# Reordering the weight preparation around the first chain of powers, and moving Wo's low half

## The chip, the cores and the metric

One core of a Trainium2 chip runs the whole kernel. The metric is the device time of one execution, in microseconds. The profiled execution, from which all rows come, is one more execution of the same kernel.

## What is computed

The input x is 4 batches of 512 tokens by 512 numbers, the context 4 by 512 by 256. In short:

```python
q = ln(heads(layernorm(x) @ Wq + bq))            # 16 heads of 32
k, v = heads(y_main @ Wk + bk), heads(y_main @ Wv + bv)      # 496 context tokens
kd, vd = heads(y_dca @ Wkv_dca + bkv_dca)                    # the last 16 tokens
x = x + (attn(q, ln(k), v) + attn(q, ln(kd), vd)) @ Wo + bo
h = silu(layernorm(x) @ lut[gate_idx].T) * (layernorm(x) @ lut[up_idx].T)
x = x + h @ lut[down_idx].T                       # inner width 1376, lut of 16 numbers
```

Every head of q and k is normalised over its 32 numbers, so there are sixteen inverse roots for each token.

## The kernel before

**Precision.** Each matrix product runs in two halves: an operand is a float16 high part plus a float16 low part, and three products (high by high, high by low, low by high) are summed. So every weight is first centred where a head norm follows (Wq, Wk and the key half of Wkv_dca: VectorE sums the heads and subtracts the mean), then converted to the high half by ScalarE, then its low half is made by a subtraction on VectorE (`low`) or, for Wv, on POOL (`values_low`, lines 495 to 498).

**The engines** run one program each, written out in order. Semaphores connect them, and whatever stands behind a waiting instruction on its engine waits too. `core` (each engine has one) is a batch's attention in numbered slots, and `between(slot)` or `prepare(slot)` hangs other work into the slots:

- Slots 0 to 8 are the projections. Eight units u (four query tiles, then the key tiles 1, 2, 3, 0) each go: TensorE `project(u)`; ScalarE `square`; VectorE `variance` (a sum for each head, L861); POOL `rstd(u)` (the power -1/2, L524); VectorE `normalise` (L867); TensorE `turn_heads` (four transposes, L1231); ScalarE `rescale` (L634, L636); VectorE `low_half` (L876). In slot u TensorE issues project(u+1), then turn_heads(u-1). VectorE issues variance(u+1), normalise(u), low_half(u-1), then the slot's extra. POOL issues rstd(u+1) and then its extra. Unit 7 is key tile 0: its 16 first tokens are the separate ones, so it takes 14 key matmuls and 12 value matmuls, a copy of the context split in two (POOL's `split_context`, whose ready signal is c0_set), and both halves of Wkv_dca (L1207, wait for wd_lo).
- Slots 9 to 40 (S_ONE on) are the first score stage: 32 pairs of heads, for the row maxima (VectorE L918, L919) and the sums of exponentials (ScalarE L664).
- Slots 41, 42 make the shifts, and slots 43 to 58 (S_TWO on) are the second score stage, 16 of them: transposed scores, exponentials (ScalarE L690), products with the values (TensorE L1305), and the norm and turn of the next batch's x.

**The lookups.** During batch 0 the FFN's weights are built from the indices, in 33 chunks. The indices come as int32 into four staging buffers (SP: `load_idx`), POOL casts a block of three chunks to float16 (`convert`, L464), SP stores it in HBM (`store_idx`) and, once a buffer is free, loads the index block four further on, then reads each chunk back in the shape needed (`load_rep`). VectorE makes four one-hot arrays of a chunk (L780), TensorE multiplies by the table (`look_up`, L1154), ScalarE evacuates (L591, L592). One chunk goes with every second slot of the first score stage, then one with each slot of the second. `load_rep(c)` waits until the one-hot set of chunk c-2 is made. EARLY says how many blocks are cast and stored before the first copies are read: POOL's `prepare` (L555) casts blocks 0 and 1 in slots 4 and 5 and the rest from S_ONE on, one for each slot.

SP's queue after its first loads (lines 346 to 364) is:

```python
for it in range(STAGES): load_idx(it)
for it in range(EARLY):  store_idx(it)
load_rep(0); load_rep(1)
sp.wait_ge(s["wd_lo"], 1)
sp.dma_start(st_o.rearrange("p (k n) -> p k n", k=G), by_chunk("Wo")).then_inc(s["wo_in"], 16)
for c in range(2, NCH):
    if EARLY + c - 2 < IT: store_idx(EARLY + c - 2)
    ...
    load_rep(c)
```

POOL begins with four requests for the lookup table (L430), then constants (lines 431 to 448), the roots for the first x tiles, the selectors, the table's constants, Wv's low half, the root for x tile 2, and then its core. In POOL's core, `split_context` stands in slot 2 behind rstd(3), and `shift_patterns` (three casts, L477 to L479) at S_ONE + 2.

Batches 1 and 2 run in a loop with the FFN of the batch before hung into the slots. Batch 3 and its FFN follow it.

## Time and profile before

| | us |
|---|---|
| median of 3 runs | 907.59 |
| lowest and highest | 905.56, 909.68 |
| the profiled execution's own time | 908.92 |
| span of the profiled execution | 907.1 |
| mean granted TensorE clock in it | 0.964 |
| TensorE matmuls busy | 799.5 (88%) |
| VectorE busy | 522.1 (58%) |
| ScalarE busy | 487.4 (54%) |
| POOL busy | 240.8 (27%) |

The own time is what the device counts for the execution, the span what the profiler's records cover. Shares of busy time are means over stages with different limits. The granted clock is TensorE's, in parts of 2.4 GHz. In the rows, PE is TensorE, DVE VectorE, ACT ScalarE, and an arrow in square brackets names what ended the idle time that stands before it. In tile names, `arena` is a large buffer that is cut into many tiles, `ps` is PSUM.

### The profile page before, as it was taken

Reading aid. Unit: us, or ns where it says so; the run is one execution under the profiler, and the core shown is the slowest. Engines: PE = TensorE matmul, PEld = TensorE weight load, DVE = VectorE, ACT = ScalarE, POOL = GpSimd, SP = SyncE. Lnnn points to the kernel's source line nnn. Section 1 sums busy time; section 2 is a strip of 40 time slices with the busy share of each in tenths; the row PEclk is TensorE's granted clock in tenths of the full one; section 3 lists DMA queues with packets and bytes.
Section 4 is the critical chain, followed back from the end, with each engine's and each line's share of the span. In section 5 each row is a group of like instructions: output and inputs, shape, how many; then the busy total and the mean of one; then the engine's idle time right before and its main releaser. Section 6 shows DMA issues by size and latency. Waiting matters only on the chain.

```text
span 907.1 us, 15618 instructions
## 1 busy us (share of the span) xinstructions
PE 799.5 (88%) x5892; PEld 319.0 (35%) x5892; DVE 522.1 (58%) x934; ACT 487.4 (54%) x964; POOL 240.8 (27%) x284
## 2 busy tenths in 40 slices
PE   3756666699889999999899999999999999979998
PEld 1321122233345333332444333334443332234443
DVE  7759999687564888221646984216458940052220
ACT  3456567677335788554246886652558865511100
POOL 7693100000156222100472222003732210002320
PEclk9986688899999999999999999999999999999999
DMA  8349844354400000112000000101000000000001
GB/s 266 98 135 293 222 131 111 90 143 117 134 1 0 2 1 1 36 47 59 26 1 1 1 1 24 48 24 47 1 1 1 1 24 25 24 24 1 1 7 40
DMA packets 45098, 50.08 MB, mean 55 GB/s; under 512 B 5984, under 2 KB 33120, under 8 KB 45024
## 3 DMA queue, kind: packets, MB, share of 16 engines
q1 hardware_dynamic: 44688, 48.81, 18.5%
q8 instruction: 49, 0.80, 0.4%
q10 hardware_dynamic: 208, 0.26, 0.1%
q14 instruction: 25, 0.20, 0.1%
q0 software_dynamic: 128, 0.00, 0.0%
HBM read 40.61 MB, written 8.45 MB: 54 GB/s over the span
## 4 chain that ended last, share of the span: by engine, by line
PE 41%; issue 26%; DVE 17%; POOL 7%; ACT 7%; DMA 1%; DVEq 0%; POOLq 0%; SPq 0%; ACTq 0%
PE ps L1108 29%; DVE arena L780 5%; DVE nmax L918 4%; PE ps L1305 3%; PE ps L1288 3%; PE ps L1261 3%; ACT ps L664 3%; POOL hrstd L524 2%; ACT arena L690 2%; POOL xrstd L492 1%; POOL arena L487 1%; PE ps L1154 1%; DVE arena L919 1%; DMA arena<-in_x 1%; DVE stat L811 1%
## 5 line engine op out<-in xcount | busy, mean ns | idle before, releaser
L1108 PE MATMUL ps<-arena,wf_hi 128*128 128x512 f16 (+1 forms) x704 | 211.9, 383 | 4.3 <-DVE arena L787 1.6
L664 ACT ACTIVATE ps<-ps,nmax 128x496 f32<-128x496 f32 x256 | 165.0, 645 | 67.1 <-DVE arena L919 66.0
L690 ACT ACTIVATE arena<-ps 128x1024 f32<-128x1024 f32 x128 | 125.4, 1023 | 78.9 <-PE ps L1294 78.8
L918 DVE TENSOR_REDUCE nmax<-ps 128x2 f32<-128x992 f32 x128 | 151.9, 1187 | 22.7 <-PE ps L1261 22.7
L1108 PE MATMUL ps<-arena,wf_lo 128*128 128x512 f16 (+1 forms) x352 | 134.2, 381 | 0.0
L524 POOL TENSOR_TENSOR hrstd<-hvar,mhalf 128x16 f32<-128x16 f32 x32 | 93.8, 2932 | 134.1 <-DVE hvar L861 134.0
L1108 PE MATMUL ps<-wf_hi,arena 128*128 128x512 f16 (+1 forms) x352 | 114.1, 380 | 0.1
L1108 PEld LDWEIGHTS ps<-arena,wf_hi 128*128 128x128 f16 (+1 forms) x704 | 66.5, 100 | 93.0 <-DVE arena L787 11.1
L780 DVE TENSOR_SCALAR arena<-arena,wf_lo 128x2048 f16<-128x2048 f16 (+1 forms) x132 | 94.1, 779 | 6.3 <-DMA arena<-idx 3.7
L1154 PE MATMUL ps<-arena,wf_lo 128*32 128x512 f16 (+1 forms) x1056 | 76.5, 432 | 22.8 <-ACT wf_lo L592 21.2
L492 POOL TENSOR_TENSOR xrstd<-xvar,mhalf 128x1 f32<-128x1 f32 x32 | 18.0, 564 | 267.4 <-DVE xvar L816 267.2
L1261 PE MATMUL ps<-arena 32*128 32x512 f16 x768 | 56.9, 401 | 22.5 <-ACT ps L664 11.5
L618 ACT ACTIVATE arena<-ps 128x512 f32<-128x512 f32 x32 | 19.2, 599 | 96.3 <-PE ps L1108 95.2
L1305 PE MATMUL ps<-arena 128*32 128x512 f32 x512 | 68.2, 604 | 0.0
L1108 PE MATMUL ps<-wf_lo,arena 128*128 128x512 f16 (+1 forms) x176 | 66.7, 379 | 0.0
L422 POOL TENSOR_TENSOR idle<-mhalf 128x1 f32<-128x1 f32 x52 | 10.0, 193 | 204.9 <-DVE arena L795 204.4
L800 DVE SCALAR_TENSOR_TENSOR arena<-ps,arena 128x512 f32<-128x512 f32 x16 | 11.1, 692 | 87.3 <-PE ps L1108 87.3
L1108 PE MATMUL ps<-wq,arena 128*128 128x512 f16 x192 | 47.4, 397 | 14.5 <-DVE arena L867 6.5
L1108 PEld LDWEIGHTS ps<-wf_hi,arena 128*128 128x128 f16 (+1 forms) x352 | 34.3, 97 | 69.0 <-issue 31.6
L599 ACT ACTIVATE arena<-ps 128x512 f32<-128x512 f32 (+1 forms) x44 | 26.4, 601 | 56.9 <-PE ps L1108 56.9
L1288 PE MATMUL ps<-arena 32*128 32x512 f16 x768 | 52.9, 378 | 3.6 <-ACT arena L690 3.6
L1154 PEld LDWEIGHTS ps<-arena,wf_lo 128*32 128x32 f16 x1056 | 27.8, 106 | 72.5 <-ACT wf_lo L592 35.0
(135 smaller groups left out, 1027.4 us busy)
## 6 DMA issues: line engine op xcount, KB each, us to landing
arena<-idx SPq DMA_DIRECT2D x124, 128.0 KB, 2.8
arena<-in_x SPq DMA_DIRECT2D x32, 256.0 KB, 2.9
wf_lo<-in_idx SPq DMA_DIRECT2D x10, 512.0 KB, 5.6
out<-arena SPq DMA_DIRECT2D x16, 256.0 KB, 2.0
idx<-wf_hi SPq DMA_DIRECT2D x10, 384.0 KB, 3.2
wf_lo<-in_idx SPq DMA_DIRECT2D x11, 256.0 KB, 6.3
arena<-in_ctxT SPq DMA_DIRECT2D x4, 512.0 KB, 5.0
arena<-in_Wq SPq DMA_DIRECT2D x4, 256.0 KB, 6.7
```

The costliest lines, as they stand in the source:

```text
L492: pool.tensor_tensor(xrstd[:, kind - 1, i:i + 1], xvar[:, kind - 1, i:i + 1], mhalf[:, 0:1], ALU.pow).then_inc(s[f"rstd{kind}"], 1)
L524: pool.tensor_tensor(hrstd[:, u % 2, :], hvar[:, u % 2, :], mhalf[:, :], ALU.pow).then_inc(s["hrstd_set"], 1)
L599: act.activation(sg[it % 2][0:m, :], ps[0:m, FB, :], ACT.Tanh, scale=0.5 / WS).then_inc(s["tanh_set"], 1)
L664: last = act.activation(sc, sc, ACT.Exp, bias=nmax[:, 0, t, h:h + 1], accum_out=den[:, 0, t, h:h + 1])
L690: act.activation(probs[n_ % 2][:, 2 * p:2 * p + 2, :], ps[:, bank:bank + 2, :], ACT.Exp).then_inc(s["probs_set"], 1)
L780: dve.tensor_scalar(l_oh[q][:, 0:n_], l_rep[c % 2][:, 0:n_], l_j[:, q:q + 1], None, ALU.is_equal)\
L918: dve.tensor_reduce(nmax[:, 0, t, 2 * p:2 * p + 2], sc[:, :, DCA:S], AX_X, ALU.max, negate=True)
L1108: last = pe.matmul(dst, l, r, start=(first and i == 0), stop=(stop and i == len(todo) - 1))
L1154: last = pe.matmul(ps[g * 32:(g + 1) * 32, FB + a_, 0:w], l_c[a_][:, q, :], l_oh[q][:, g * w:(g + 1) * w], start=(q == 0), stop=(q == NJ - ...
L1261: last = pe.matmul(ps[:, pair_bank(m + j // 2) + j % 2, :], qT[x_][of_head(j), g, cols], kT[y_][of_head(j), g, :], start=(k == 0), stop=(k ...
L1288: pe.matmul(ps[:, SC + j, :], kT[x_][of_head(j), g, cols], qT[y_][of_head(j), g, :], start=(k == 0), stop=False)
L1305: last = pe.matmul(ps[j * HD:(j + 1) * HD, AB, :], v_sb[:, kt, h * HD:(h + 1) * HD], probs[n_ % 2][:, j, :], start=(kt == 0), stop=(kt == ...
```

## The change

Each engine's list is reordered. No arithmetic is added or removed.

- SP: Wq's third block is loaded ahead of x tile 1. One block instead of two is stored ahead of the first copies. Wo's load waits for two signals of wd_lo (Wkv_dca's low half is now in two parts).
- POOL: the requests for the table stand behind the constants. Wv's low half moves behind rstd(1), the split of the context behind rstd(4). Block 0 is cast in slot 1, block 1 in slot 8, blocks 2 to 10 from slot 9 on, and the shift patterns in slot S_ONE + 12.
- ScalarE: Wv's high half moves behind b's. The turn of x tile 3 stands ahead of Wk's high half. Wkv_dca's conversion is in slot 3 instead of 2. The wait for the value bias moves to Wo's conversion.
- VectorE: the low half of x tile 0 stands earlier. The sums and centring of Wk stand later, with the low half of x tile 3 between. Wk's low half is in slot 0. Wkv_dca's low half is made in two parts in slots 4 and 5 instead of whole in slot 3. Wo's low half is in slot S_TWO + 2 instead of S_ONE + 8.
- TensorE: unit 7 waits for both parts of Wkv_dca's low half.

```diff
-STAGES, EARLY = 4, 2
+STAGES, EARLY = 4, 1
@@ SP
-                if k == 1:
+                if k == 2:
                     load_x(1, tile_of(flat, xaddr(0, 0, 1)), x_first[1])
...
-            sp.wait_ge(s["wd_lo"], 1)
+            sp.wait_ge(s["wd_lo"], KC)
@@ POOL
-            for r in range(NR4):
-                pool.dma_start(lut_w[r * 32:(r + 1) * 32, :], row("lut", r * NJ, (r + 1) * NJ).to_broadcast([32, NJ])).then_inc(s["lut_in"], 16)
             pool.memset(mhalf[:, :], -0.5).then_inc(s["ident_set"], 1)
...
             pool.memset(caug[:, :, :, :, :, :].rearrange("p t j e w c -> p (t j e w c)"), 0.0).then_inc(s["caug_zero"], 1)
+            for r in range(NR4):
+                pool.dma_start(lut_w[r * 32:(r + 1) * 32, :], row("lut", r * NJ, (r + 1) * NJ).to_broadcast([32, NJ])).then_inc(s["lut_in"], 16)
...
-                    if u == 2:
+                    if u == 3:
                         split_context(a)
...
             lookup_constants()
-            values_low()
             norm(1, 2, (0, 0))
             def prepare(slot):
-                if 4 <= slot < 4 + EARLY:
-                    convert(slot - 4)
-                if slot == S_ONE + 2:
+                if slot == 0:
+                    values_low()
+                if slot == 1:
+                    convert(0)
+                if NU <= slot < NU + IT - EARLY:
+                    convert(EARLY + slot - NU)
+                if slot == S_ONE + 12:
                     shift_patterns()
-                if S_ONE <= slot < S_ONE + IT - EARLY:
-                    convert(EARLY + slot - S_ONE)
@@ ScalarE
                 if prev is None:
                     act.wait_ge(s["par_set"], 1)
-                    act.wait_ge(s["bvs_set"], 1)
...
             query_hi(1)
+            query_hi(2)
             turn(1, 1, (0, 0), LB0[1])
-            act.wait_ge(s["wv_in"], 16)
-            act.activation(fl(wv[0]), st_kv[1], ACT.Copy, scale=WS).then_inc(s["wv_hi"], 1)
-            query_hi(2)
             query_hi(3)
             act.activation(b16[:, :], st_b, ACT.Copy, scale=WS).then_inc(s["b_hi"], 1)
+            act.wait_ge(s["wv_in"], 16)
+            act.activation(fl(wv[0]), st_kv[1], ACT.Copy, scale=WS).then_inc(s["wv_hi"], 1)
...
             turn(1, 2, (0, 0), LB0[2])
+            turn(1, 3, (0, 0), LB0[3])
             act.wait_ge(s["wk_cent"], 1)
             act.activation(fl(wk[0]), st_kv[0], ACT.Copy, scale=WS).then_inc(s["wk_hi"], 1)
-            turn(1, 3, (0, 0), LB0[3])
             def prepare(slot):
-                if slot == 2:
+                if slot == 3:
                     act.wait_ge(s["wd_cent"], 1)
...
                 if slot == S_ONE + 3:
+                    act.wait_ge(s["bvs_set"], 1)
                     act.wait_ge(s["wo_in"], 16)
@@ VectorE
-            moments(1, 1, first, x_first[1])
             query_centre(1)
             query_low(0)
+            moments(1, 1, first, x_first[1])
+            turn(1, 0, first, LB0[0])
             query_sums(2)
             standardise(1, 1, first, x_first[1], x_first[1])
             query_centre(2)
             query_low(1)
-            turn(1, 0, first, LB0[0])
...
             standardise(1, 2, first, x_first[2], x_first[2])
-            dve.wait_ge(s["wk_in"], 16)
-            dve.tensor_reduce(sum_k, key, A-_-, ALU.add).then_inc(s["wk_sum"], 1)
             moments(1, 3, first, x_first[3])
             variance(first, 1)
             turn(1, 2, first, LB0[2])
+            standardise(1, 3, first, x_first[3], x_first[3])
+            normalise(first, 0, True)
+            dve.wait_ge(s["wk_in"], 16)
+            dve.tensor_reduce(sum_k, key, A+_+, ALU.add).then_inc(s["wk_sum"], 1)
+            turn(1, 3, first, LB0[3])
             dve.wait_ge(s["wk_sum"], 1)
             dve.scalar_tensor_tensor(out=key, in0=spread(sum_k), scalar=-1.0 / HD, in1=key, op0=ALU.mult, op1=ALU.add).then_inc(s["wk_cent"], 1)
-            standardise(1, 3, first, x_first[3], x_first[3])
-            normalise(first, 0, True)
...
-            turn(1, 3, first, LB0[3])
-            dve.wait_ge(s["wk_hi"], 1)
-            low(fl(wk[1]), st_kv[0], fl(wk[0])).then_inc(s["wk_lo"], 1)
...
                 if slot == 0:
                     dve.tensor_tensor(bvs[:, :], bvm, bvd, ALU.add).then_inc(s["bvs_set"], 1)
+                    dve.wait_ge(s["wk_hi"], 1)
+                    low(fl(wk[1]), st_kv[0], fl(wk[0])).then_inc(s["wk_lo"], 1)
...
-                if slot == 3:
+                if slot in (4, 5):
                     dve.wait_ge(s["wd_hi"], 1)
-                    low(wd[1][:, :, :], st_d, wd[0][:, :, :]).then_inc(s["wd_lo"], 1)
-                if slot == S_ONE + 8:
+                    k = slot - 4
+                    low(wd[1][:, k, :], st_d[:, k, :], wd[0][:, k, :]).then_inc(s["wd_lo"], 1)
+                if slot == S_TWO + 2:
                     dve.wait_ge(s["wo_hi"], 1)
                     low(fl(wo[1]), st_o, fl(wo[0])).then_inc(s["wo_lo"], 1)
@@ TensorE, unit 7
-                            pe.wait_ge(s["wd_lo"], 1)
+                            pe.wait_ge(s["wd_lo"], KC)
```

## Rows read from the trace of the kernel before

**Rows 1.** Stages: us; busy of PE, PEld, DVE, ACT, POOL; clock, DMA, GB/s.

```profile
68.50:161.00 92.50, 56.21 (x672) 17.51 (x672) 90.99 (x139) 61.51 (x162) 11.30 (x8) 0.77 0.66 185
...
170.00:238.90 68.90, 64.46 (x928) 22.36 (x928) 53.14 (x92) 53.69 (x76) 2.21 (x4) 1.00 0.45 121
...
238.90:907.10 668.20, 636.51 (x4075) 259.73 (x4075) 326.67 (x597) 339.38 (x677) 174.66 (x210) 0.99 0.06 19
```

**Rows 2.** Timeline of POOL, front: start us, us, line, operation.

```profile
1.26 2.21 POOL L430 DMA_DIRECT2D wf_lo<-in_lut  x4 [0.82 <-POOLq L1355]
...
20.64 1.49 POOL L497 TENSOR_SCALAR arena<-arena 128x1024 f32<-128x1024 f32 x1
...
22.21 2.12 POOL L498 TENSOR_TENSOR wv<-arena,wv 128x1024 f16<-128x1024 f32 x1
...
28.26 2.91 POOL L524 TENSOR_TENSOR hrstd<-hvar,mhalf 128x16 f32<-128x16 f32 x1
...
38.22 5.83 POOL L524 TENSOR_TENSOR hrstd<-hvar,mhalf 128x16 f32<-128x16 f32 x2 [7.05 <-DVE hvar L861]
...
46.90 2.91 POOL L524 TENSOR_TENSOR hrstd<-hvar,mhalf 128x16 f32<-128x16 f32 x1 [0.36 <-DVE hvar L861]
...
54.38 1.46 POOL L464 CAST wf_hi<-wf_lo 128x1536 f16<-128x1536 int32 x1
...
60.52 3.34 POOL L524 TENSOR_TENSOR hrstd<-hvar,mhalf 128x16 f32<-128x16 f32 x1
```

**Rows 3.** Timeline of VectorE, front.

```profile
24.89 0.55 DVE L821 TENSOR_SCALAR arena<-arena,mv,xrstd 128x512 f32<-128x512 f32 x1 [1.79 <-POOL xrstd L492]
...
34.50 0.69 DVE L833 TENSOR_TENSOR arena<-ps,arena 128x512 f16<-128x512 f32 x1 [2.67 <-ACT arena L603]
...
37.44 0.70 DVE L861 TENSOR_REDUCE hvar<-arena 128x16 f32<-128x528 f32 x1
...
48.55 2.29 DVE L967 SCALAR_TENSOR_TENSOR wd<-arena,wd 128x2048 f16<-128x2048 f32 x1
...
55.07 1.32 DVE L876 TENSOR_TENSOR arena<-arena 128x512 f16<-128x512 f32 x1
```

**Rows 4.** Timeline of TensorE, front.

```profile
28.84 4.34 PE L1108 MATMUL ps<-wq,arena 128*128 128x512 f16 x12 [2.69 <-DVE arena L833]
...
35.25 2.76 PE L1108 MATMUL ps<-wq,arena 128*128 128x512 f16 x12 [0.98 <-DVE arena L833]
...
47.47 0.66 PE L1231 MATMUL ps<-ident,arena 128*128 128x128 f32 x4 [1.97 <-DVE arena L867]
...
64.64 1.12 PE L1231 MATMUL ps<-ident,arena 128*128 128x128 f32 x4 [4.06 <-DVE arena L867]
```

**Rows 5.** Two windows of one us: columns as in rows 1.

```profile
30.00:31.00 1.00, 1.00 (x4) 0.36 (x3) 1.00 (x3) 1.00 (x1) 1.00 (x1) 0.50 0.04 10
...
32.00:33.00 1.00, 1.00 (x6) 0.39 (x4) 0.00 (x0) 0.00 (x0) 0.00 (x0) 0.97 0.00 0
```

**Rows 6.** Timelines of VectorE and POOL, first score stage.

```profile
72.41 2.73 DVE L780 TENSOR_SCALAR arena<-arena,wf_lo 128x2048 f16<-128x2048 f16 x4
...
77.44 3.90 DVE L780 TENSOR_SCALAR arena<-arena,wf_lo 128x2048 f16<-128x2048 f16 x4
...
77.35 1.47 POOL L464 CAST wf_hi<-wf_lo 128x1536 f16<-128x1536 int32 x1 [5.66 <-DMA wf_lo<-in_idx]
...
95.29 2.28 DVE L967 SCALAR_TENSOR_TENSOR wo<-arena,wo 128x2048 f16<-128x2048 f32 x1
...
97.49 1.18 DVE L918 TENSOR_REDUCE nmax<-ps 128x2 f32<-128x992 f32 x1
```

**Rows 7.** Line 780, 77.4 to 81.2: ns least, median, most.

```profile
L780 DVE TENSOR_SCALAR arena<-arena,wf_lo x4: 737/742/1919, 77.4 to 80.6; 128x2048 f16<-128x2048 f16 x4
```

**Rows 8.** Timelines of VectorE and TensorE, second score stage.

```profile
181.28 2.73 DVE L780 TENSOR_SCALAR arena<-arena,wf_lo 128x2048 f16<-128x2048 f16 x4
...
187.07 2.49 PE L1154 MATMUL ps<-arena,wf_lo 128*32 128x512 f16 x32
```

More of the change, by code:

```diff
@@ L1025, in _ @@
             standardise(1, 2, first, x_first[2], x_first[2])
-            dve.wait_ge(s["wk_in"], 16)
-            dve.tensor_reduce(sum_k, key, AX_X, ALU.add).then_inc(s["wk_sum"], 1)
             moments(1, 3, first, x_first[3])
@@ L1030, in _ @@
             turn(1, 2, first, LB0[2])
+            standardise(1, 3, first, x_first[3], x_first[3])
+            normalise(first, 0, True)
+            dve.wait_ge(s["wk_in"], 16)
+            dve.tensor_reduce(sum_k, key, AX_X, ALU.add).then_inc(s["wk_sum"], 1)
+            turn(1, 3, first, LB0[3])
             dve.wait_ge(s["wk_sum"], 1)
             dve.scalar_tensor_tensor(out=key, in0=spread(sum_k), scalar=-1.0 / HD, in1=key, op0=ALU.mult, op1=ALU.add).then_inc(s["wk_cent"], 1)
-            standardise(1, 3, first, x_first[3], x_first[3])
-            normalise(first, 0, True)
             dve.wait_ge(s["ln_in"], 16 * len(PARAMS))
```

## The prediction

> **What bounds the kernel now.** I read the stages first, then each engine's timeline in the stretches that the change touches. The stages [rows 1] show that the edited program (batch 0 and the lookups) is 238.9 us of 907.1, and that TensorE is 64.46 of 68.9 us busy in the second score stage and 636.51 of 668.2 us behind it. That last stretch is untouched. In the first score stage (68.5 to 161) VectorE is busy 90.99 of 92.5 us, and it is the bound. In front of it runs the chain of powers on POOL. From rstd(2) on, each of the two engines waits for the other by turns.
>
> The powers take 2.9 us each [rows 2]. The third starts only at 38.22, after a wait of 7.05 for VectorE's sum, itself at 37.44 [rows 3]. The sixth ends at 54.38, where the first index cast starts. The eighth starts at 60.52 and ends at 63.86, and the first scores follow at 68.5 [rows 1].
>
> **The sum, part 1: the front.** The lut requests (2.21 us on POOL [rows 2]) leave the head, but x0's root must still pass them: I take 0, at most 2.2 gained. The reordered Wq2/x1 loads and the earlier x turn shift VectorE by under 1 us. The real gain is Wv's low half (1.49 + 2.12 us [rows 2]) leaving the path of rstd of x2: the step behind that root waited 1.79 us for it, until 24.89 [rows 3], and can now run near 22.4. Following VectorE's new order with unchanged durations, projection 2 can start at about 25.95 rather than 28.84, and x3's low half at about 30.2 rather than 34.50 [rows 3].
>
> Between that low half and the sum for rstd(2) there were 2.94 us of VectorE work (34.50 to 37.44). Now Wk's centring (1.13) and the parameters (0.9) come on top, with about 1 us of waiting for ScalarE's conversion of Wk. The sum's end would be at 36.1, 2.0 earlier than 38.14. But Wv's low half now starts on POOL when rstd(1) ends, about 28.8, and its two-input step runs from 30.4 to 32.5, just when the centring of Wk wants to start. In the row at 55.07 a VectorE step with two SBUF inputs took 1.32 instead of 0.68 us, until the cast of 54.38 (1.46) had ended [rows 2, 3]. By that the centring waits until 32.5 and the sum ends at 37.8. If projection 2 finds the low clock (12 matmuls in 4.34 rather than 2.76 us [rows 4], 0.50 granted, which is 1.2 GHz [rows 5]) it also ends at about 37.7. I take 37.8; bounds 36.1 and 38.2.
>
> From there POOL has rstd(2), the conversion of block 0 (1.46), rstd(3), rstd(4), the split of the context, rstd(5). The split took 2.5 us, from 44.05 (the two powers from 38.22) to 46.54, which is 46.90 less its wait of 0.36. With hand-offs that is 4 x 2.9 + 1.46 + 2.6 = 15.7, so rstd(5) ends at 53.5 (bounds 51.8 and 53.9), against 54.38. All their inputs come earlier: the costliest is ScalarE's Wkv_dca conversion, now a slot later, and I find the fifth sum ready near 47.4 while POOL is free near 50.7.
>
> Now the new wait. Projection 7 (the mixed tile) waits for both parts of Wkv_dca's low half, and the second stands in slot 5, behind normalise(5), which waits for rstd(5). The whole low half was 2.29 us and ended at 50.84, ahead of need [rows 3]. Now: 0.05 + 0.6 (normalise) + 0.6 (low half 4) + 1.15 = 2.4 us after rstd(5), about 55.9, TensorE may start. It will have been idle for over 6 us. After 4.06 idle four transposes took 1.12 us, after 1.97 idle 0.66 [rows 4]. The projection's 14 key matmuls cost 3.2 us at the rate of the row at 35.25 (2.76 for 12) and about 4.8 us if the first 3.2 us are at half rate, as in the row at 28.84, where 0.50 was granted until about 32 [rows 4, 5]. I take 4.9 with hand-off: they end at 60.8. ScalarE's square 0.65, VectorE's sum 0.75, and rstd(7) starts at 62.3: later than 60.52, though its two casts are gone from between. The values' 12 matmuls (2.6), transposes, ScalarE's rescales of units 5, 6 (1.35 each) and 7 (1.9) and VectorE's low halves between them put the scores 9.3 us after the keys' end: 70.1. Casts of blocks 1 to 4 run on POOL right then and may hold a low half back by 0.6 (it did at 55.07). **Front: +1.7** (scores at 70.2); the ends are 66.8 (-1.7: 51.8 and the high clock) and 71.4 (+2.9: every low half held).
>
> **Part 2: first score stage.** VectorE loses Wo's low half: 97.49 - 95.29 = -2.2 us, all of it on the bound [rows 6]. Its cover is full: no idle is shown from 72.4 to 161. What comes on: a one-hot set of four takes 2.73 us alone and 3.90 when an index cast runs beside it (77.35 against 77.44) [rows 6]. A single instruction of it then takes 1.92 instead of 0.74 [rows 7]. Four of the five casts after 72.41 collided (sets of 77.44, 83.66, 89.91, 99.02); the fifth, at 103.85, ended before 105.27. So 4 x 1.2 = 4.8 us lie in this stage today. With EARLY at 1, load 5 is issued one chunk later and so are those behind it. The casts in this stage become 5 to 10, six, and the three casts of the shift patterns (0.6, 0.2 and 1.0 us, in front of the stage till now) come behind the tenth. A load is issued when a set has ended, and its cast starts 9 to 10 us after that end; a cycle is 2.4 + 2.65 to 3.9, so two cycles later the next set is under way: the phase makes collisions the rule. I take 0.6 for the first, 5 x 1.2 for the rest and 0.5 of the patterns: 7.1 against 4.8, **+2.3**, bounds -4.8 (none) and +3.9 (8.7 in all). SP's other moves (Wo behind the second part of Wd's low half, one store fewer ahead of the first copies) leave the first copies earlier, at about 44, and nothing waits for them: a set could not start before its slot.
>
> **Part 3: second score stage.** The 2.2 us of Wo's low half now stand ahead of the set that ran 181.28 to 184.01 [rows 8]. TensorE's lookup of 187.07 took 2.49 rather than 1.91 us: it is already at VectorE's heels, and otherwise dense [rows 1, 8]. With the set 2.2 later the lookup in front of it ends about 1.4 late, the set of 186.16 and its lookup 2.0 late. TensorE has no gap behind to win it back, and transfers start from the sets, so they shift too. **+2.0**; bounds 0 and 2.2. The 79 per cent busy VectorE speaks for 0; where it is idle it waits for TensorE, so I stay near 2.
>
> ScalarE's wait for bvs moves to a slot where it is long met: 0. Sum: +1.7 - 2.2 + 2.3 + 2.0 = **+3.8 us**. On the profiled execution's 908.9 that is 912.7; on the median of the three runs, 907.6 (the profiled one is 1.3 above it), 911.4. I forecast 911.4. A measurement tells about 0.5 per cent, 4.5 us.
>
> **A page on it.** The Trainium skill, "SBUF — State Buffer", section "Who interferes with whom", says that VectorE and GpSimd share one port pair as an exclusive lock: fast-mode and two-input VectorE work and GpSimd's reads shut each other out for whole instructions. By that rule whatever of the moved casts meets such work costs its full length, the patterns' casts and the low halves of the tail too, and the sum would be that of the first rival, 914.2; the rows at 55.07 and 77.44 agree with it for the casts that they show [rows 3, 6].
>
> **The rivals.** *Lock everywhere (slower)*: place, the casts. If loads land so that every cast and pattern meets a set, and the tail's low halves too, front +2.9 and stage one +3.9 - 2.2, stage two +2.0: +6.6, 914.2, over the bound. For it: four collisions of five today. Against: the fifth missed. It decides from about five collisions plus the patterns on.
> *The chain leads (no change)*: Wk's centring starts before POOL's step (it misses by 0.4 us), and TensorE's clock stays high: front -1.7, else as forecast: +0.4, 908.0. Against: six idle microseconds before projection 7.
> *Casts miss (faster)*: no cast meets a set: 4.8 saved, -2.2, +2.0, +1.7 = -3.3, 904.3; with the chain leading as well 900.9, past the bound on the other side. For it: the phase depends on when the loads land, and the cast of 103.85 missed. Against: 4 of 5.
> *Wo hidden*: the second stage absorbs it: 909.4.
> The change can hardly fail to do what it says: each line moves work in a fixed order.
>
> **How the numbers follow.** Forecast 0.45; lock everywhere 0.25; chain leads 0.12; casts miss 0.10 (half of that past the bound); Wo hidden 0.08. The range for eight in ten runs from the chain-leads case less the runs' own scatter of 2 us, 905.5, to the lock case and as much, 916. Slower by over 0.5 per cent: the lock case nearly whole and a quarter of the forecast's, 0.34. Faster: 0.08. Same: 0.58.
>
> **What would show it.** Right: rstd(2) near 37.8; TensorE idle over 5 us before the 14 matmuls of projection 7, at a granted clock of 0.50, with Wkv_dca's second low half just before; rstd(7) after 62; first scores at 70; six 1.9-us one-hot instructions in stage one; a lookup 2 us late from 187 on. Wrong: scores before 68, fewer than four long one-hots, or the stage from 170 no longer than 68.9 us.

## The result, and the profile after

| | before | changed |
|---|---|---|
| median of the runs | 907.18 (14 runs) | 914.54 (14 runs) |
| lowest to highest | 902.45 to 909.68 | 910.18 to 917.63 |
| span of the first trace | 907.1 | 910.1 |
| span of a second trace | 904.1 | 916.0 |

The ratio is 1.0079 with a 95% interval of 1.0061 to 1.0096: slower by 7.3 us, 0.8 per cent. The slowest run of the kernel before (909.68) still lies below the fastest of the changed one (910.18). The forecast was 911.4 in a range of 905.5 to 916.

Three places on TensorE cut the run into stages: the first scores, the four transposes of the shifts (at the end of the first score stage), and the first projection of the second batch. TensorE's timeline of the changed kernel, with the key matmuls of unit 7 ahead of them:

```profile
55.12 2.72 PE L1110 MATMUL ps<-wk,arena 128*128 128x512 f16 x6 [5.30 <-DVE wd L968]
...
57.63 2.27 PE L1110 MATMUL ps<-wd,arena 128*128 128x512 f16 x6
...
71.84 1.47 PE L1263 MATMUL ps<-arena 32*128 32x512 f16 x12 [3.44 <-DVE arena L877]
...
166.51 0.58 PE L1278 MATMUL ps<-ident_h,caug 128*128 128x128 f16 x4 [7.88 <-DVE caug L942]
...
241.48 2.76 PE L1110 MATMUL ps<-wq,arena 128*128 128x512 f16 x12 [1.37 <-ACT wf_lo L593]
```

The same places in the kernel before:

```profile
52.59 1.46 PE L1108 MATMUL ps<-wk,arena 128*128 128x512 f16 x6
...
68.51 1.47 PE L1261 MATMUL ps<-arena 32*128 32x512 f16 x12 [2.75 <-DVE arena L876]
...
165.09 0.58 PE L1276 MATMUL ps<-ident_h,caug 128*128 128x128 f16 x4 [7.88 <-DVE caug L941]
...
238.96 2.76 PE L1108 MATMUL ps<-wq,arena 128*128 128x512 f16 x12 [1.37 <-ACT wf_lo L592]
```

With the second traces of both (runs `after_again` and `before_again` below), the stages last, in us:

| | front | first score stage | second score stage | rest |
|---|---|---|---|---|
| before | 68.5, 66.2 | 96.6, 94.9 | 73.9, 73.8 | 668.1, 669.2 |
| changed | 71.8, 73.6 | 94.7, 97.5 | 75.0, 75.8 | 668.6, 669.1 |
| difference of the means | +5.4 | +0.3 | +1.6 | +0.2 |

The sum, +7.5, is what the medians show. One pair of traces alone would have misled: the first pair gives +3.0. Two other runs that share the changed kernel's whole front, `wo_back` and `sp_early2`, have it at 73.4 and 73.3.

**The front.** VectorE's timeline of the changed kernel: the centring of Wk, the second part of Wkv_dca's low half, and the last three low halves of the projections:

```profile
29.18 2.87 DVE L1036 SCALAR_TENSOR_TENSOR arena<-arena 128x1024 f32<-128x1024 f32 x1
...
53.75 1.22 DVE L968 SCALAR_TENSOR_TENSOR wd<-arena,wd 128x1024 f16<-128x1024 f32 x1
...
64.92 1.71 DVE L877 TENSOR_TENSOR arena<-arena 128x512 f16<-128x512 f32 x1 [2.63 <-ACT arena L637]
...
67.16 1.34 DVE L877 TENSOR_TENSOR arena<-arena 128x512 f16<-128x512 f32 x1
...
70.41 1.38 DVE L877 TENSOR_TENSOR arena<-arena 128x512 f16<-128x512 f32 x1 [1.91 <-ACT arena L637]
```

And POOL's: Wv's low half (second step), the third power, the eighth, the casts behind it:

```profile
28.84 2.13 POOL L498 TENSOR_TENSOR wv<-arena,wv 128x1024 f16<-128x1024 f32 x1
...
36.23 2.90 POOL L524 TENSOR_TENSOR hrstd<-hvar,mhalf 128x16 f32<-128x16 f32 x1 [5.25 <-DVE hvar L862]
...
61.77 2.90 POOL L524 TENSOR_TENSOR hrstd<-hvar,mhalf 128x16 f32<-128x16 f32 x1 [6.39 <-DVE hvar L862]
...
64.62 6.62 POOL L464 CAST wf_hi<-wf_lo 128x1536 f16<-128x1536 int32 x4
```

The third power starts at 36.23, 2.0 earlier than the 38.22 of [rows 2], although the centring was held up: 2.87 us at 29.18, until the step of 28.84 (2.13) had ended. Against the second trace of the kernel before, where this power starts at 35.95, it is no lead at all. Whatever lead there is, it is lost. The second part of Wkv_dca's low half ends at 54.97, and only then do unit 7's key matmuls start, at 55.12. They take 2.72 and 2.27 us for six each where they took 1.46 before. TensorE had stood idle for 5.30 us, and the clock granted to it is 0.50, which is 1.2 GHz. Its windows say so (columns as in rows 1, the clock is the third from the end):

```profile
55.00:57.00 2.00, 1.89 (x5) 0.74 (x6) 0.00 (x0) 0.00 (x0) 0.38 (x1) 0.50 0.41 49
57.00:59.00 2.00, 2.00 (x6) 0.70 (x5) 0.00 (x0) 0.00 (x0) 0.00 (x0) 0.50 0.93 345
```

The eighth power waits until 61.77. Behind it four casts run from 64.62, and the three low halves beside them take 1.71, 1.34 and 1.38 us instead of 0.7.

**The first score stage.** VectorE's timeline of the changed kernel, three sets of one-hot arrays:

```profile
80.79 2.73 DVE L781 TENSOR_SCALAR arena<-arena,wf_lo 128x2048 f16<-128x2048 f16 x4
...
99.50 2.74 DVE L781 TENSOR_SCALAR arena<-arena,wf_lo 128x2048 f16<-128x2048 f16 x4 [2.22 <-DMA arena<-idx]
...
105.66 2.74 DVE L781 TENSOR_SCALAR arena<-arena,wf_lo 128x2048 f16<-128x2048 f16 x4 [1.03 <-DMA arena<-idx]
```

The long sets of [rows 6] are gone: all but one (3.10 at 116.72) take the plain 2.73 us in the first trace, where 4.8 us of blocking had been (two sets, of 3.24 and 3.04 us, are longer in the second trace). Instead three sets wait for their copies, 3.7 us in all (2.22, 1.03, 0.43), and in the second trace four sets, 5.4. SP's queue shows why, load 5's second part and then the next requests:

```profile
66.97 0.70 SPq L312 DMA_DIRECT2D wf_lo<-in_idx  x1
...
78.50 2.86 SPq L330 DMA_DIRECT2D arena<-idx  x4
...
92.26 3.03 SPq L312 DMA_DIRECT2D wf_lo<-in_idx  x1
```

SP issued nothing from 67.7 to 78.50. The store of block 2 and load 6 stood behind the copies of chunk 2, which wait for the first set. The windows show the transfers (columns as in rows 1; the last two are the DMA share and GB/s):

```profile
71.80:78.40 6.60, 3.72 (x36) 0.91 (x40) 5.06 (x9) 2.73 (x8) 1.47 (x1) 0.50 0.00 0
78.40:105.00 26.60, 16.13 (x208) 5.35 (x204) 23.56 (x39) 18.16 (x46) 4.08 (x3) 0.85 0.98 259
```

Nothing moves for 6.6 us, and then the DMA engines are full for 26 (a share of 0.98). The issue of one kind of request (line 312) grows as well, from 0.70 us at 66.97 to 3.03 at 92.26.

**The second score stage.** VectorE's timeline, Wo's low half and the set behind it, and TensorE's, the two lookups that use this set and the next:

```profile
182.92 2.28 DVE L968 SCALAR_TENSOR_TENSOR wo<-arena,wo 128x2048 f16<-128x2048 f32 x1
...
185.12 2.73 DVE L781 TENSOR_SCALAR arena<-arena,wf_lo 128x2048 f16<-128x2048 f16 x4
...
186.02 2.51 PE L1156 MATMUL ps<-arena,wf_lo 128*32 128x512 f16 x32 [0.81 <-DVE arena L781]
...
190.90 2.51 PE L1156 MATMUL ps<-arena,wf_lo 128*32 128x512 f16 x32 [0.40 <-DVE arena L781]
```

Both lookups waited for VectorE. In the kernel before only the second of the two was held ([rows 8]), and by half a microsecond.

### The profile page after: what moved, and what is told of

Its sections match the earlier page's. It is cut to its first block, busy times and chain, and to the rows that moved or that the text cites. A ratio compares the mean times of both kernels' runs of the same rounds, so it can differ in the third digit from the quotient of the medians.

```text
span 910.1 us, 15619 instructions
## 1 busy us (share of the span) xinstructions
PE 802.8 (88%) x5892; PEld 320.6 (35%) x5892; DVE 522.2 (57%) x935; ACT 487.1 (54%) x964; POOL 238.5 (26%) x284
## 4 chain that ended last, share of the span: by engine, by line
PE 42%; issue 26%; DVE 14%; ACT 8%; POOL 6%; DMA 2%; SPq 1%; DVEq 0%; POOLq 0%; ACTq 0%
PE ps L1110 30%; ACT ps L664 4%; PE ps L1307 3%; PE ps L1290 3%; PE ps L1263 3%; DVE arena L781 3%; DVE nmax L919 2%; POOL hrstd L524 2%; PE ps L1156 2%; ACT arena L690 2%; POOL xrstd L492 1%; DMA wf_lo<-in_idx 1%; POOL arena L487 1%; PE ps L1233 1%; DVE stat L812 1%
## 5 line engine op out<-in xcount | busy, mean ns | idle before, releaser
L664 ACT ACTIVATE ps<-ps,nmax 128x496 f32<-128x496 f32 x256 | 165.2, 646 | 66.2 <-DVE arena L920 65.0
L1110 PEld LDWEIGHTS ps<-arena,wf_hi 128*128 128x128 f16 (+1 forms) x704 | 66.6, 101 | 93.3 <-DVE arena L788 11.0
L781 DVE TENSOR_SCALAR arena<-arena,wf_lo 128x2048 f16<-128x2048 f16 (+1 forms) x132 | 89.6, 740 | 9.3 <-DMA arena<-idx 6.9
L1263 PE MATMUL ps<-arena 32*128 32x512 f16 x768 | 55.6, 393 | 23.4 <-ACT ps L664 11.7
L1307 PE MATMUL ps<-arena 128*32 128x512 f32 x512 | 68.2, 604 | 0.0
L422 POOL TENSOR_TENSOR idle<-mhalf 128x1 f32<-128x1 f32 x52 | 10.1, 194 | 205.1 <-DVE arena L796 204.6
L1290 PE MATMUL ps<-arena 32*128 32x512 f16 x768 | 53.5, 381 | 3.3 <-ACT arena L690 3.3
L1156 PEld LDWEIGHTS ps<-arena,wf_lo 128*32 128x32 f16 x1056 | 28.0, 106 | 71.8 <-ACT wf_lo L593 31.2
```

Of the source, the lines that this page charges most:

```text
L664: last = act.activation(sc, sc, ACT.Exp, bias=nmax[:, 0, t, h:h + 1], accum_out=den[:, 0, t, h:h + 1])
L781: dve.tensor_scalar(l_oh[q][:, 0:n_], l_rep[c % 2][:, 0:n_], l_j[:, q:q + 1], None, ALU.is_equal)\
L1110: last = pe.matmul(dst, l, r, start=(first and i == 0), stop=(stop and i == len(todo) - 1))
L1156: last = pe.matmul(ps[g * 32:(g + 1) * 32, FB + a_, 0:w], l_c[a_][:, q, :], l_oh[q][:, g * w:(g + 1) * w], start=(q == 0), stop=(q == NJ - ...
L1263: last = pe.matmul(ps[:, pair_bank(m + j // 2) + j % 2, :], qT[x_][of_head(j), g, cols], kT[y_][of_head(j), g, :], start=(k == 0), stop=(k ...
L1290: pe.matmul(ps[:, SC + j, :], kT[x_][of_head(j), g, cols], qT[y_][of_head(j), g, :], start=(k == 0), stop=False)
```

## The experiments

All times are medians; the ratio is to the kernel before, run on the same chip, with its 95% interval.

**`after_again`, `before_again`: no edit.** For the changed kernel:

> The changed kernel once more, for a second trace and a joint comparison. The median of its runs was 7.3 us over the kernel before (914.5 against 907.2), while its trace shows only 3.0 us (span 910.1 against 907.1): front +3.3, first score stage -1.9, second +1.1, rest +0.5. Theory A (the trace shown is a lucky execution: the first stage's collisions and copy waits differ from one execution to the next): this trace shows a front within 0.5 us of the last and a first stage several us longer. Theory B (the difference lies elsewhere, in the loop and the last batch): the first stage again lasts 94.7 us, and the rest behind the second stage differs. Time: about 914.

Measured: 915.4 (1.0080, 1.0057 to 1.0104), span 916.0. Stage one lasts 97.5 instead of 94.7, as theory A has it. But the front is not the same within 0.5 us: it is 1.8 longer. TensorE's timeline of this trace:

```profile
56.03 2.72 PE L1110 MATMUL ps<-wk,arena 128*128 128x512 f16 x6 [6.58 <-DVE wd L968]
...
58.54 2.77 PE L1110 MATMUL ps<-wd,arena 128*128 128x512 f16 x6
...
73.64 1.47 PE L1263 MATMUL ps<-arena 32*128 32x512 f16 x12 [3.43 <-DVE arena L877]
```

The second part of Wkv_dca came 0.9 us later, and twelve matmuls rather than some ten ran at the low clock (2.72 and 2.77). The 0.9 us arose on POOL: beside VectorE's two-input steps at 48.64 and 49.44, the last step of the split took 0.65 us instead of 0.22, and rstd(5) 3.87 instead of 3.34. For the kernel before:

> The kernel before once more, for a second trace of it. Its one trace (span 907.1) lies 1.7 us above what its median of 907.2 stands for (the own time is 1.8 above the span), and the changed kernel's two traces (910.1 and 916.0) lie 2.6 below and 3.2 above the median's 912.8. Theory, the casts' phase varies from execution to execution: this trace has the same front (first scores within 0.5 us of 68.5), but fewer than four long one-hot sets or a first stage other than 96.6 us by over 1. Rival, the kernel before is regular and the kernels differ elsewhere: again four long sets, first stage 96.6, and the whole within 1 us of 907.1.

Measured: 906.45 (1.0006, 0.9988 to 1.0024), span 904.1. One long set instead of four, a wait of 1.4 for a copy, and stage one 94.9: the phase of the casts does vary within one kernel. The front varies too, which was not expected: here the step behind the third x tile's root, the third power and the unit 7 keys stand at

```profile
22.86 0.55 DVE L821 TENSOR_SCALAR arena<-arena,mv,xrstd 128x512 f32<-128x512 f32 x1 [0.66 <-POOL xrstd L492]
```

```profile
35.95 5.83 POOL L524 TENSOR_TENSOR hrstd<-hvar,mhalf 128x16 f32<-128x16 f32 x2 [6.81 <-DVE hvar L861]
```

```profile
50.32 1.46 PE L1108 MATMUL ps<-wk,arena 128*128 128x512 f16 x6
...
66.23 1.47 PE L1261 MATMUL ps<-arena 32*128 32x512 f16 x12 [2.75 <-DVE arena L876]
```

against 24.89 in [rows 3], 38.22 in [rows 2], and 52.59 and 68.51 above. In the first trace VectorE waited 1.44 us for the second x tile, until 10.27; in this one it did not wait. So single traces of this front differ by about 2 us.

**`wo_alone`: the kernel before with one edit.**

```diff
-                if slot == S_ONE + 8:
+                if slot == S_TWO + 2:
                     dve.wait_ge(s["wo_hi"], 1)
```

> The kernel before, with Wo's low half moved to the third slot of the second score stage and nothing else. Theory, saturated second stage: the first stage is 2.2 us shorter, the second 2.0 to 2.4 us longer, total within 1 us of the kernel before. Rival, the second stage hides it: total 2 us below. Rival, collisions: taking 2.2 us out shifts the one-hot sets against the casts, and the number of 1.9-us one-hot instructions changes from 4: 1.2 us for each.

Measured: 906.72 (1.0000, 0.9979 to 1.0020): no change in the sum. In the trace the second stage is 75.8, 1.9 over the 73.9 before, and the first 92.2, with one long set and 1.4 us of waits for copies. The second stage, TensorE's timeline:

```profile
180.00 2.51 PE L1154 MATMUL ps<-arena,wf_lo 128*32 128x512 f16 x32 [0.82 <-DVE arena L780]
...
184.88 2.51 PE L1154 MATMUL ps<-arena,wf_lo 128*32 128x512 f16 x32 [0.40 <-DVE arena L780]
```

Two lookups wait for VectorE as in the changed kernel. The saturated second stage is shown in the traces (`wo_back` below has it the other way round), and the rival of hiding falls.

**`wo_back`: the changed kernel with the same edit undone.**

> The changed kernel with Wo's low half back in the first score stage. Theory (VectorE bounds the one stage, TensorE the other): first stage +2.2, second -2.2 (from 75.0 and 75.8 to about 73.7), total as the changed kernel within 1 us, 914 to 915. Rival, copies: since sets wait up to 5.4 us for their copies in the changed kernel's first stage, Wo's low half can hide in such a wait; then the first stage gains under 1 us and the total falls by 2, to 912.5.

Measured: 913.14 (1.0065, 1.0048 to 1.0082), 1.4 to 2.3 below the two medians of the changed kernel. The second stage falls to 73.5, the cleanest number here. Stage one is 97.3, with no set waiting for a copy and five sets held by casts. It lies within the changed kernel's own scatter (94.7, 97.5), so how much of Wo's low half hides there isn't settled. The two medians differ by about what they are uncertain.

**`wd_slot4`: the changed kernel, both parts of Wkv_dca's low half in slot 4.**

```diff
-                if slot in (4, 5):
+                if slot == 4:
                     dve.wait_ge(s["wd_hi"], 1)
-                    k = slot - 4
-                    low(wd[1][:, k, :], st_d[:, k, :], wd[0][:, k, :]).then_inc(s["wd_lo"], 1)
+                    for k in range(KC):
+                        low(wd[1][:, k, :], st_d[:, k, :], wd[0][:, k, :]).then_inc(s["wd_lo"], 1)
```

> The changed kernel, but both parts of Wkv_dca's low half in slot 4, so that the second no longer stands behind the fifth power. Theory, the front's loss is the wait of unit 7's projection for that part: TensorE's idle of 5.3 us before those matmuls falls under 3, they end before 56 instead of 60.3, the eighth power follows the seventh at once, and the first scores stand 5 to 6 us earlier, at about 66; total 5 us below the changed kernel, about 909 to 910. Rival, the chain of powers is held elsewhere (VectorE's order): scores earlier by under 2 us.

Measured: 907.79 (1.0009, 0.9993 to 1.0024): one edit takes back 6.8 us of the 7.3, and the kernel stands level with the one before. TensorE's timeline:

```profile
52.13 2.56 PE L1110 MATMUL ps<-wk,arena 128*128 128x512 f16 x6 [2.39 <-DVE wd L968]
...
54.49 2.08 PE L1110 MATMUL ps<-wd,arena 128*128 128x512 f16 x6
...
68.51 1.46 PE L1263 MATMUL ps<-arena 32*128 32x512 f16 x12 [3.43 <-DVE arena L877]
```

TensorE's idle fell to 2.39, the keys started 3 to 4 us earlier, and the scores 3.3 to 5.1 earlier (68.51). So that much of the 6.8 is shown in the front; where the rest went the traces don't settle, as stage one was 94.3 here (3.0 us of waits for copies) and 94.7 and 97.5 there. The scores were expected at 66. The keys ended at 56.8, later than the 56 expected, since they still met the low clock, and the eighth power, at 58.45, did not follow the seventh at once: POOL waited 2.87 us for it.

**`wd_as_before`: Wkv_dca's conversion in slot 2 and its low half in slot 3.**

```diff
 ScalarE
-                if slot == 3:
+                if slot == 2:
                     act.wait_ge(s["wd_cent"], 1)
 VectorE
-                if slot in (4, 5):
+                if slot == 3:
```

(the low half as in `wd_slot4`)

> The changed kernel with Wkv_dca's conversion on ScalarE in slot 2 and its whole low half on VectorE in slot 3, as before the change. Theory, wait plus clock: the part is ready near 49, unit 7's 14 key matmuls follow the fifth transposes without an idle of over 1 us and take 3.2 us at the full clock instead of 5.2, the last two powers follow one another and end near 59.6, scores start at 65 to 66 (71.8 and 73.6 in the two traces of the changed kernel); total 6 to 8 us below the changed kernel, 907 to 909. The price is ScalarE's conversion ahead of the fifth square: the fifth power starts 1 to 2 us later. Rival: that price is the reason for the new place and eats the gain: scores after 69.

Measured: 909.72 (1.0032, 1.0012 to 1.0052), 5 us below the changed kernel. The scores stand at 68.97, so the clock half of the theory failed here. The part was ready at 49.5, yet TensorE's timeline has

```profile
52.58 2.65 PE L1110 MATMUL ps<-wk,arena 128*128 128x512 f16 x6 [1.09 <-issue]
```

TensorE did wait, 1.24 us ahead of the fifth transposes and 1.09 behind them. What held it was not Wkv_dca but POOL's split of the context, which ended at 52.48: ScalarE's conversion had pushed the fifth power to 45.56 (43.6 in `wd_slot4`) and the split behind it, and beside VectorE's two-input steps the split itself took 4.1 us instead of 2.5. That is the price in the expectation, only it was paid at another wait.

**`index_back`: the changed kernel with the index work as before.**

```diff
-STAGES, EARLY = 4, 1
+STAGES, EARLY = 4, 2
-                if slot == 1:
-                    convert(0)
-                if NU <= slot < NU + IT - EARLY:
-                    convert(EARLY + slot - NU)
-                if slot == S_ONE + 12:
+                if 4 <= slot < 4 + EARLY:
+                    convert(slot - 4)
+                if slot == S_ONE + 2:
                     shift_patterns()
+                if S_ONE <= slot < S_ONE + IT - EARLY:
+                    convert(EARLY + slot - S_ONE)
```

> The changed kernel with the index work as before: EARLY 2, blocks 0 and 1 cast in slots 4 and 5, the rest and the shift patterns from the first score stage on. Theory, the index order costs the first stage (late copies: waits of 2.2, 1.0 and 0.4 us for the copies in the changed trace; casts on VectorE's port): total 2 to 4 us below the changed kernel. In the front, the cast of block 0 leaves the chain behind the third power but two casts come between the sixth and eighth: scores within 1.5 us of 71.8, as unit 7 still waits for Wkv_dca. Rival, the index order is neutral: total within 1.5 us of the changed kernel.

Measured: 911.35 (1.0049, 1.0031 to 1.0067), 3 to 4 us below. The scores are at 71.1 and stage one lasts 93.3, with one wait of 1.6 for a copy. Against the two traces of the changed kernel the front is 0.8 and 2.6 us shorter and stage one 1.4 and 4.2.

**`sp_early2`: the changed kernel, SP's order alone as before.**

```diff
-STAGES, EARLY = 4, 1
+STAGES, EARLY = 4, 2
-                if NU <= slot < NU + IT - EARLY:
-                    convert(EARLY + slot - NU)
+                if NU <= slot < NU + IT - 1:
+                    convert(1 + slot - NU)
```

> The changed kernel, casts in its places, but SP stores two blocks (not one) ahead of the first copies, as before the change. In the changed trace the transfers stand wholly still from 71.8 to 78.4, because the store of block 2 and load 6 are queued behind the copies of chunk 2, which wait for the first one-hot set; after that they are saturated to 105 and sets wait 3.7 us (5.4 in the second trace) for copies. Queue theory: with one block more ahead of that wait the transfers work before 78, the sets wait under 2 us, the first stage lasts 92 to 94.5 us, total 2 to 3 us below the changed kernel, 912. Rival, the casts' own places cost (in the run with the whole index order undone): no gain here, 914 to 915. Risk: the first copies now wait for block 1's cast at about 66.

Measured: 914.76 (1.0071, 1.0049 to 1.0092): no gain. The DMA engines do work in the same stretch behind the first scores,

```profile
73.30:79.90 6.60, 3.73 (x36) 0.92 (x40) 5.06 (x9) 2.73 (x8) 1.47 (x1) 0.50 1.11 271
```

a share of 1.11 instead of 0.00, the waits for copies fall to 2.6 us, and stage one lasts 94.5. But they stay full for the 26 us behind it as well, and the total doesn't move. The idle DMA engines are a real effect of the queue's order; filling them alone gained nothing that the medians show. Its rest was 671.0, 2 us over all other traces, for which I have no cause.

**`wd4_index_back`: both repairs.** The edits of `wd_slot4` and `index_back` together.

> Both repairs together: the low half of Wkv_dca in slot 4 and the index work as before. If the two costs are independent: the two gains add up (7 and 4 us against the changed kernel), total 903 to 905, below the kernel before; scores start near 67.7, first stage 93 to 94. If they are one and the same (the casts' place only mattered through the front's wait): no more than 1 us below the kernel with slot 4 alone, 907.

Measured: 908.11 (1.0004, 0.9985 to 1.0023). The gains don't add up: 907.8 with the first repair alone, 908.1 with both. The front is 68.2, and stage one, with three waits for copies (4.4 us), 95.5. That fits an index order which costs only while the front is held by unit 7, but it isn't shown: the difference between the two gains, 3 us, is about as large as its uncertainty, and the two kernels ran on different chips.

**`wd4_casts_late`: `wd_slot4`, and POOL holds its casts back.**

```diff
+                if slot == NU:
+                    pool.wait_ge(s["tr_lo"], NU)
                 if NU <= slot < NU + IT - EARLY:
                     convert(EARLY + slot - NU)
```

> The kernel with Wkv_dca's low half in slot 4, and POOL waits for VectorE's last low half of the projections before it casts block 1. This takes the casts away from beside the last three low halves (1.71, 1.34, 1.37 us each there, 0.68 alone). Port theory: all three take 0.7, scores start 1.5 to 2 us earlier (66.6 instead of 68.5). The price: blocks 1 to 4 are cast and stored 6 us later, so in the first stage more sets may wait for their copies or meet casts: stage one 94.3 plus 0 to 3. Total within 2 us of 907.8. Rival: the low halves are slow for another cause: they stay over 1.3 us and the scores do not move.

Measured: 909.53 (1.0026, 1.0013 to 1.0040), 1.7 over `wd_slot4`. VectorE's timeline, the last three low halves and the first set; and POOL's, the casts:

```profile
59.53 0.69 DVE L879 TENSOR_TENSOR arena<-arena 128x512 f16<-128x512 f32 x1 [1.41 <-ACT arena L639]
...
60.90 0.68 DVE L879 TENSOR_TENSOR arena<-arena 128x512 f16<-128x512 f32 x1
...
64.16 0.69 DVE L879 TENSOR_TENSOR arena<-arena 128x512 f16<-128x512 f32 x1 [2.57 <-ACT arena L639]
...
68.81 5.33 DVE L783 TENSOR_SCALAR arena<-arena,wf_lo 128x2048 f16<-128x2048 f16 x4
```

```profile
64.91 6.15 POOL L464 CAST wf_hi<-wf_lo 128x1536 f16<-128x1536 int32 x4 [4.65 <-DVE arena L879]
```

All three low halves take 0.69: the port theory is shown. But the first set then takes 5.33 us, 2.6 over its own, and of the later ones two more are held clearly (4.50 and 3.93 us). The blocking moved from one place to the other, and stage one lasts 97.5. The front itself shrank by 3.6 us, to 64.9, more than the low halves explain. TensorE's timeline:

```profile
51.76 1.45 PE L1112 MATMUL ps<-wk,arena 128*128 128x512 f16 x6 [3.03 <-POOL arena L512]
...
53.05 1.46 PE L1112 MATMUL ps<-wd,arena 128*128 128x512 f16 x6
...
64.90 1.47 PE L1265 MATMUL ps<-arena 32*128 32x512 f16 x12 [2.75 <-DVE arena L879]
```

Here unit 7's keys ran at the full clock after an idle of 3.03 us. That and a start 0.4 us earlier bring the value matmuls behind them to 54.77 instead of 56.83, 2.1 us of the 3.6. From there to the first scores it takes 10.1 us instead of 11.7, and these 1.6 us are what the casts beside the low halves cost. Only two of the three holds lie on the path: behind the middle one VectorE waits for ScalarE anyway (1.91 us in the changed kernel).

**`casts_in_gaps` and `gaps_wo_back`: the attempt at a better kernel.** From `wd_slot4`:

```diff
-STAGES, EARLY = 4, 1
+STAGES, EARLY = 4, 2
                 if slot == 0:
                     values_low()
-                if slot == 1:
                     convert(0)
-                if NU <= slot < NU + IT - EARLY:
-                    convert(EARLY + slot - NU)
+                if slot == 5:
+                    convert(1)
+                    convert(2)
+                if NU <= slot < NU + IT - 3:
+                    convert(3 + slot - NU)
```

> From the kernel with Wkv_dca's low half in slot 4: EARLY 2; block 0 is cast right behind Wv's low half (POOL stood still from 31.0 to 36.2 there), blocks 1 and 2 behind the seventh power (where POOL waits 2.9 us for unit 7), the rest from slot 8 on. Port theory: fewer casts beside the last low halves, no cast in the chain: scores at 66 to 67 (68.5 there). Queue theory: blocks 4 to 6 are loaded before the first set, so the sets wait under 2 us, first stage 92 to 94. Second stage 76 as in the others with Wo there. Total 903 to 906, 1 to 4 us below the kernel before. Rival: block 0's cast holds Wk's and the context's low halves on VectorE and the third power starts after 37.5; then the front gains nothing, total 907.

> The same with Wo's low half in the first score stage. If transfers bound the first stage, Wo's low half hides in the wait for copies: first stage longer by under 1.5 us, second 2.2 shorter, total 1 us below the run with Wo in the second stage. If VectorE bounds it: first stage +2.2, total equal. Together 902 to 906.

(the second has Wo's low half in slot S_ONE + 8.) Measured: 910.29 (1.0028, 1.0006 to 1.0051) and 907.97 (1.0011, 0.9990 to 1.0032). The first scores stand at 68.98 and 66.66, stage one lasts 93.4 and 94.6, stage two 75.8 and 73.6. No set waited more than 0.3 us for a copy in either, so the queue theory holds for the waits. But casts held sets again (to 4.26 and 3.94 us in the first trace, 3.24 and 3.34 in the second), and the block 0 cast held VectorE (a step of 0.35 us took 1.61, at 31.93), so that the third power started at 37.2 instead of 36.2. The traces' spans, 905.8 and 903.0, lie 2.7 and 3.2 below what the medians stand for: they are lucky executions, and the medians decide. No kernel here beats the one before by more than can be told.

The two kernels are the same up to the first score stage, and yet their fronts differ by 2.3 us. TensorE's timelines of unit 7's keys, the first kernel's and the second's:

```profile
53.28 2.22 PE L1112 MATMUL ps<-wk,arena 128*128 128x512 f16 x6 [2.30 <-DVE wd L970]
...
55.30 2.42 PE L1112 MATMUL ps<-wd,arena 128*128 128x512 f16 x6
```

```profile
52.23 1.46 PE L1112 MATMUL ps<-wk,arena 128*128 128x512 f16 x6 [2.30 <-DVE wd L970]
...
53.52 1.46 PE L1112 MATMUL ps<-wd,arena 128*128 128x512 f16 x6
```

After the same idle of 2.30 us one execution met the low clock and the other didn't. That is 1.7 us of the 2.3, and it is an accident of the execution, not a property of the kernel.

## Why the prediction was right, and where it was not

**The front, forecast +1.7, measured +5.4 (means of two traces each).** The chain as written down came true at nearly every station behind the fifth power, in the first trace. The centring of Wk was blocked (32.5 forecast as its start, 29.18 with 2.87 us measured, the same place in the order). Rstd(5) ended at 52.4 or 53.4 by the steps behind it (53.5 forecast). Unit 7 started at 55.1 and 56.0 (55.9), its keys ended at 60.3 and 62.1 (60.8), and the eighth power started at 61.8 and 63.6 (62.3). `wd_slot4` shows the wait for the second part as the main cause: with it placed one slot earlier the first scores come 3.3 to 5.1 us sooner and the median falls by 6.8.

The start was off: the third power stood at 36.2, not 37.8, since everything up to it was 1.6 us earlier than I had it. The first root passed the table's requests sooner than I allowed (x0's standardised step at 6.40), and the second x tile wasn't later for its new place in the queue. The conversion of block 0, two powers back to back at 3.1 each, the split and rstd(5) took 16.3 us where I had 15.7, so that 1.0 of the 1.6 us was left at the end of rstd(5), and 0.8 at the start of unit 7 (none in the second trace).

The term that was mis-sized is the tail: "Casts of blocks 1 to 4 run on POOL right then and may hold a low half back by 0.6". I let it count for 0.1. Three low halves were held, by 1.0, 0.65 and 0.7, and from the keys' end to the first scores it took 11.5 us in both traces, not 9.3. Of these 2.2 us, 1.6 are the casts' by `wd4_casts_late`, where each low half takes 0.69 once the casts are away; the other 0.6 I had summed too short. The Trainium skill ("SBUF — State Buffer", "Who interferes with whom") says that a VectorE instruction with two SBUF inputs contends with a GpSimd instruction that reads SBUF. The traces agree: 1.71, 1.34 and 1.38 us beside the casts. A further part is not the change's: the one trace that I had of the kernel before had a slow front, 68.5 where the other has 66.2, and that alone puts 1.1 us on the difference of the means. With 0.4 us of later keys (61.2 on the mean, 60.8 forecast) this makes up the 3.7 us between +1.7 and +5.4.

**The first score stage, forecast +0.1, measured +0.3: right in size, wrong in its making.** The step that failed is "the phase makes collisions the rule". I had six casts and the patterns cost 7.1 us on the one-hot sets. They cost 0.4 in the first trace and under 1 in the second: by my own list, fewer than four long one-hots was a sign of being wrong, and there were one and two. The gain from that was given back as a new wait that I had looked for and dismissed: I wrote that the first copies come earlier and that nothing waits for them. True of chunks 0 and 1. But EARLY at 1 puts a store and a load behind the copies of chunk 2, so the transfers pause and later chunks come late, by 3.7 and 5.4 us in all. `sp_early2` fills the pause and halves the waits, `casts_in_gaps` removes them; both then meet casts again. In the traces VectorE's collisions with casts and its waits for copies tend to trade with one another (five sets held and no wait in `wo_back`; none held and 4.4 us of waits in `wd4_index_back`). That a held set gives the copies time is my explanation; no run tests it. That the measured +0.3 lies so near the forecast +0.1 is luck.

**The second score stage, forecast +2.0, measured +1.6.** The lookups of 187 and after are late as described, and by 2.4 us in the first trace. 1.3 of that came back at the very end, where the last set waits for its copy: 2.73 us before, 1.41 after. Cleaner are `wo_alone` (+1.9) and `wo_back` (-1.9 on the mean of 75.4): Wo's low half costs in the one stage what it saves in the other, and moving it alone is worth nothing that can be told, 1.0000.

**The whole.** The sign, the wait of unit 7 and the second stage were right, the first stage right by luck, and the sum too small by half: +3.8 forecast, +7.3 measured. The rival "lock everywhere" had the time, 914.2, and half of the mechanism: in the tail of the front it was so (71.4 forecast), in the score stage it was not. Its point of decision, five collisions and the patterns, was not reached.

## What to carry to other kernels

When work is split into parts and spread over slots of an in-order engine, price its last part by the wait that it now stands behind, not by its length: 1.2 us of Wkv_dca behind one more power put the first scores 3.3 to 5.1 us later. A step moved out from under a critical chain takes its port and its queue along, so ask what it will run beside and what is queued behind it. Where executions of one kernel scatter by 1% and one pair of traces differs by 3 us while the medians differ by 7, take a second trace of each before explaining anything.

## What was not expected of the hardware

- The clock that TensorE finds after a pause doesn't follow from the pause alone. Unit 7's keys met 1.2 GHz after 2.39 us of idle in `wd_slot4` and in `wd_as_before` behind 1.24 idle, four transposes and 1.09, but 2.4 GHz after 3.03 us in `wd4_casts_late`. After 2.30 us they met 1.2 GHz in `casts_in_gaps` and 2.4 GHz in `gaps_wo_back`, with the same program up to there. The price is 1.7 to 2.9 us on 14 matmuls. Why it differs is open.
- POOL's casts and VectorE's one-hot instructions block each other in turn, one instruction at a time. In `wd4_casts_late` the cast in progress at 68.81 and the next two ran beside the first set. The set took 5.33 us instead of 2.73, and these next two casts, 1.47 us each when alone, took 1.92 and 1.70.
- Issuing a request on SP can take far longer while the DMA engines are full, and so delay the very queue that feeds them: that of line 312 took 0.70 us at 66.97 in the changed kernel, and 3.03 at 92.26, at a DMA share of 1.10. Full engines alone don't decide it: at 82.36 the same request took 0.77 us at a share of 1.08, and that of line 311 just ahead of the slow one took 0.43. What does is open.
